# Rows of x in an interleaved order in an attention kernel, so that one DMA transpose turns a step's queries

## The reference, cut to what matters

```python
x: (4, 1024, 512)
xn = layernorm(x)
c_Q  = rms_norm(xn @ Wq_down);  c_KV = rms_norm(xn @ Wkv_down)
q_nop, q_pe = c_Q @ Wq_up, c_Q @ Wq_pe        # 16 heads of 128 and of 64 (rotary)
k_nop, v = split(c_KV @ Wkv_up)               # 8 key/value heads, each for 2 query heads
k_pe = rms_norm(xn @ Wk_pe)                   # rotary, one for all heads
scores = (q . k) * 192**-0.5, causal mask, softmax
y = attn @ v;  attn_out = y @ Wo
x_q = ternary(xn), w = ternary(weight) + rram;  ffn = x_q @ w.T
return x + attn_out + ffn
```

## Time and profile before

| | |
|---|---|
| median of 3 runs | 1703.25 us (1702.78 to 1703.85) |
| the profiled execution | 1702.12 us, span 1700.3 us |
| PE busy | 1633.8 us, 96% of the span |
| DVE, ACT, POOL busy | 1301.6, 1104.3, 580.3 us |
| DMA | 254.58 MB, mean 150 GB/s; queue of SP and ACT transposes and copies 80.3% of 16 engines' span |
| granted TensorE clock | 0.997 of full speed |

### The profile page before, as it was taken

How to read it: one execution, slowest core, us unless ns; L and a number is a source line. 1 busy time by engine, 2 the same in 40 slices (tenths; PEclk the granted TensorE clock), 3 DMA queues, 4 the chain that set the end, 5 groups by cost and what they waited for, 6 DMA issues and landing times.

```text
span 1700.3 us, 30407 instructions
## 1 busy us (share of the span) xinstructions
PE 1633.8 (96%) x9612; PEld 837.1 (49%) x9612; DVE 1301.6 (77%) x3369; ACT 1104.3 (65%) x2464; POOL 580.3 (34%) x1048
## 2 busy tenths in 40 slices
PE   4789999999999999999999999999999999999999
PEld 3445455544544445545454445554455444555444
DVE  5888878768688687777868787876868868777765
ACT  5877667567576666656666566756756666666663
POOL 3323334333343233433333333433333323333320
PEclk9999999999999999999999999999999999999999
DMA  9467988879979889987969988887987988998886
GB/s 259 97 103 141 150 147 154 147 134 158 152 138 161 145 152 159 166 149 122 161 126 167 170 148 147 154 149 129 161 153 141 159 144 151 162 159 147 147 153 126
DMA packets 914889, 254.58 MB, mean 150 GB/s; under 512 B 901608, under 2 KB 904042, under 8 KB 914410
## 3 DMA queue, kind: packets, MB, share of 16 engines
q1 hardware_dynamic: 904032, 228.98, 80.3%
q10 hardware_dynamic: 9162, 17.37, 3.3%
q0 software_dynamic: 1536, 6.29, 1.1%
HBM read 19.76 MB, written 8.39 MB: 17 GB/s over the span
## 4 chain that ended last, share of the span: by engine, by line
PE 71%; DMA 9%; issue 6%; ACT 5%; DVE 5%; SPq 2%; POOL 2%; ACTq 0%; DVEq 0%; POOLq 0%
DMA FT<-F 6%; PE bank L695 5%; PE bank L693 5%; PE bank L692 5%; PE bank L694 5%; PE bank L795 5%; PE bank L794 5%; PE bank L793 5%; PE bank L737 4%; PE bank L738 4%; PE bank L739 4%; PE bank L705 4%; ACT P L1082 2%; SPq L1848 2%; DVE F L1499 2%
## 5 line engine op out<-in xcount | busy, mean ns | idle before, releaser
L1082 ACT ACTIVATE P<-P,nm 128x256 f32<-128x256 f32 (+15 forms) x512 | 381.7, 746 | 439.6 <-DVE nm L1485 439.6
L1485 DVE CUSTOM_DVE_ANT_0 P<-bank,mask,neg 128x256 f32<-128x256 f32 (+15 forms) x512 | 383.0, 783 | 270.0 <-PE bank L705 261.8
L1719 POOL TENSOR_SCALAR sn<-sm 128x1 f32<-128x1 f32 x512 | 209.0, 409 | 926.1 <-ACT P L1082 918.6
L1077 ACT ACTIVATE F<-P,rc 128x256 f16<-128x256 f32 (+15 forms) x512 | 366.7, 743 | 101.0 <-DVE rc L1493 62.4
L1499 DVE SCALAR_TENSOR_TENSOR F<-P,rc,F 128x256 f16<-128x256 f32 (+15 forms) x512 | 401.6, 796 | 2.7 <-ACT F L1077 2.3
L692 PE MATMUL bank<-K,Q 128*128 128x512 f16 (+7 forms) x760 | 241.7, 319 | 0.8 <-DMA Q<-QS 0.8
L695 PE MATMUL bank<-K,Q 128*128 128x512 f16 (+7 forms) x760 | 241.7, 319 | 0.0
L693 PE MATMUL bank<-K,Q 128*128 128x512 f16 (+7 forms) x760 | 241.7, 319 | 0.0
L694 PE MATMUL bank<-K,Q 128*128 128x512 f16 (+7 forms) x760 | 241.7, 319 | 0.0
L793 PE MATMUL bank<-WO,YH 128*128 128x512 f16 x512 | 194.3, 379 | 4.0 <-DVE YL L1505 3.7
L794 PE MATMUL bank<-WO,YH 128*128 128x512 f16 x512 | 194.0, 379 | 0.0
(11 more groups left out here) (229 smaller groups left out, 2874.8 us busy)
## 6 DMA issues: line engine op xcount, KB each, us to landing
out<-X ACTq DMA_DIRECT2D x31, 256.0 KB, 3.6
X<-in_x ACTq DMA_DIRECT2D x28, 256.0 KB, 3.5
FT<-F SPq DMA_TRANSPOSE x348, 4.4
wo<-in_Wo POOLq DMA_DIRECT2D x4, 1024.0 KB, 7.0
Q<-QS SPq DMA_TRANSPOSE x256, 3.6
V<-CC SPq DMA_DIRECT2D x32, 64.0 KB, 3.0
X<-in_x SPq DMA_DIRECT2D x4, 256.0 KB, 8.4
kv<-in_Wkv_up POOLq DMA_DIRECT2D x1, 1024.0 KB, 12.5
```

The costliest lines, as they stand in the source:

```text
L1077: return e.eng.activation(dst, src, ACT.Copy, scale=scale)
L1082: e.eng.activation(m.P[:, u % 4, 0:w], m.P[:, u % 4, 0:w], ACT.Exp, bias=m.nm[:, u % 8:u % 8 + 1], scale=-1.0, accum_out=m.sm[:, u % 8:u % ...
L1485: e.eng.tensor_tensor_reduce(out=m.P[:, u % 4, 0:w], in0=m.pS[u % 2][:, off:off + w], in1=m.mask[:, end - w:end], scale=m.neg[:, :], scala ...
```

## The change

A tile's 128 rows are put on the partitions in another order: partition 2k + a holds row 64a + k of the tile (k from 0 to 63, a = 0 or 1). This is made where x is loaded, and undone where the output is stored, by the access pattern on the DRAM side; the rotary table is loaded in the same order, by two transfers in place of one.

- One DMA transpose turns all 128 partitions of `QS` (1,536 columns) into `Q`. A side's 128 weights are then every second column of two heads' 256.
- The causal mask and the products with `V` need keys in their natural order. The turned keys land in a new buffer `KT`, and POOL copies them to `K` in natural order (`keep_keys`, at g = 3 of tile t for tile t+2, behind the two units of p = 1; twice in the prologue). Scores wait for `k_at` of that copy in place of the transfer's `k_in`. The wait for the scores that still read the old keys moves from SP to POOL; SP waits for the copy of the tile before.
- `V` gets its natural order from two transfers of 64 partitions, each reading every second partition of `CC`.
- TensorE still writes `pY` in runs of 64, in natural order. The copies `values_hi` and `values_lo` write `YH` and `YL` with a step of two columns. They no longer multiply by 2^-4; the factor is put into the sum's scale (2^-12 for 2^-15) and the output's (2^-12 for 2^-11). In `values_lo` this makes a TENSOR_TENSOR of the SCALAR_TENSOR_TENSOR.

```diff
 def rows(dram, t):
-    return dram[b, i * 128:i * 128 + 128, :]
+    return by_places(dram[b, i * 128:i * 128 + 128, :])
+def by_places(dram):
+    return dram.rearrange("(a k) n -> k a n", a=2)
+def natural(values):
+    return values.rearrange("p (h a k) -> p h a k", a=2, k=64)
+def placed(values):
+    return values.rearrange("p (h k a) -> p h a k", a=2, k=64)
...
+        self.KT = own("KT", [128, 4, 128], F16)
-        self.Q = own("Q", [128, 2, 2, 768], F16)
+        self.Q = own("Q", [128, 2, 12, 128], F16)
...
     a, g = divmod(h, 2)
-    Q = m.Q[:, n % 2, a, :]
-    return [Q[:, 256 * x + 128 * g:256 * x + 128 * g + 128] for x in range(3)]
+    Q = m.Q[:, n % 2, :, :]
+    return [Q[:, 4 * x + 2 * g:4 * x + 2 * g + 2, :].rearrange("p h q -> p (h q)")[:, a::2] for x in range(3)]
...
-        e.wait_ge(s.q_in[p][n % 2], 16 * (n // 2 + 1))
-        e.wait_ge(s.k_in, 16 * (n // NG + 1))
+        e.wait_ge(s.q_in[n % 2], 16 * (n // 2 + 1))
+        e.wait_ge(s.k_at, n // NG + 1)
...
     def values_hi(n):
-        copy(m.YH[:, n % 2, :], m.pY[n % 2], 2.0 ** -4).then_inc(s.yh, 1)
+        copy(placed(m.YH[:, n % 2, :]), natural(m.pY[n % 2])).then_inc(s.yh, 1)
...
     def values_lo(n):
-        e.eng.scalar_tensor_tensor(out=m.YL[:, n % 2, :], in0=m.pY[n % 2], scalar=2.0 ** -4, in1=m.YH[:, n % 2, :],
-                                   op0=ALU.mult, op1=ALU.subtract).then_inc(s.yl, 1)
+        e.eng.tensor_tensor(placed(m.YL[:, n % 2, :]), natural(m.pY[n % 2]), placed(m.YH[:, n % 2, :]),
+                            ALU.subtract).then_inc(s.yl, 1)
...
+    def keep_keys(self, t):
+        at = key_slot(b, i) * 128
+        e.wait_ge(s.k_in, 16 * (t + 1))
+        if b:
+            e.wait_ge(s.wom, 16)
+        if b >= 2:
+            e.wait_ge(s.s, 4 * NG * (LAST_OF[b - 2] + 1))
+        e.eng.tensor_copy(m.K[:, :, at:at + 128].rearrange("p c (a k) -> p c a k", a=2),
+                          m.KT.rearrange("p c (k a) -> p c a k", a=2)).then_inc(s.k_at, 1)
...
 def gpsimd_attention(e, m, s, tiles, queries):
+            if (g, p) == (3, 1) and t + LEAD - 1 < T:
+                tiles.keep_keys(t + LEAD - 1)
...
     def keep(self, t):
         if t >= 2:
             e.wait_ge(s.up, NG * (t - 1))
+            e.wait_ge(s.k_at, t)
         if b >= 2:
-            e.wait_ge(s.s, 4 * NG * (LAST_OF[b - 2] + 1))
             e.wait_ge(s.pv, JBASE[NG * (LAST_OF[b - 2] + 1)])
-        e.eng.dma_start_transpose(out=m.K[:, :, at * 128:at * 128 + 128],
+        e.eng.dma_start_transpose(out=m.KT[:, :, :],
                                   in_=m.CC[:, 1, :, :].rearrange("p a n -> p (a n)")).then_inc(s.k_in, 16)
-        e.eng.dma_start(m.V[:, at, :, :], m.CC[:, 1, :, 0:128]).then_inc(s.v_in, 16)
+        for a in range(2):
+            e.eng.dma_start(m.V[64 * a:64 * a + 64, at, :, :], m.CC[a::2, 1, :, 0:128]).then_inc(s.v_in, 16)
...
     def turn_queries(n):
-        for a in range(2):
-            e.eng.dma_start_transpose(out=m.Q[:, n % 2, a, :].rearrange("p (c q) -> p c q", q=64),
-                                      in_=m.QS[64 * a:64 * a + 64, n % 2, :]).then_inc(s.q_in[a][n % 2], 16)
+        e.eng.dma_start_transpose(out=m.Q[:, n % 2, :, :], in_=m.QS[:, n % 2, :]).then_inc(s.q_in[n % 2], 16)
```

More of the change, by code:

```diff
@@ L339, in __init__ @@
         self.ld_x, self.st_o, self.xt_in = sems("ld_x", XSLOTS), sem("st_o"), sem("xt_in")
-        self.c_in, self.k_in, self.v_in = sem("c_in"), sem("k_in"), sem("v_in")
+        self.c_in, self.k_in, self.v_in, self.k_at = sem("c_in"), sem("k_in"), sem("v_in"), sem("k_at")
         self.const, self.wqs, self.nwq = sem("const"), sem("wqs"), sem("nwq")
@@ L360, in __init__ @@
         self.qh, self.ql, self.ph, self.pl = sem("qh"), sem("ql"), sem("ph"), sem("pl")
-        self.q_in = [sems("q_first", 2), sems("q_second", 2)]
+        self.q_in = sems("q_in", 2)
         self.s, self.mk, self.ex, self.sm, self.rc, self.fh, self.fl = (
@@ L714, in weigh_ready @@
             e.wait_ge(s.ft_in[z % FSLOTS], 16 * (z // FSLOTS + 1))
-        e.wait_ge(s.v_in, 16 * (n // NG + 1))
+        e.wait_ge(s.v_in, 32 * (n // NG + 1))
         if n >= 2:
@@ L927, in parts_hi @@
             e.wait_ge(s.k_in, 16 * t)
-            e.wait_ge(s.v_in, 16 * t)
+            e.wait_ge(s.v_in, 32 * t)
         self.copy(m.CC[:, 0, 0, 0:192], m.CR[:, 0:192], m.RM[:, 4, 0:1])
@@ L942, in queries_hi @@
         if n >= 2:
-            e.wait_ge(s.q_in[0][n % 2], 16 * (n // 2))
-            e.wait_ge(s.q_in[1][n % 2], 16 * (n // 2))
+            e.wait_ge(s.q_in[n % 2], 16 * (n // 2))
         e.eng.activation(m.QS[:, n % 2, 0:512], m.pU, ACT.Copy).then_inc(s.qh, 1)
@@ L1102, in last_values_hi @@
         e.wait_ge(s.c, N - 2)
-        copy(m.YH[:, (N - 1) % 2, 256 * p:256 * p + 256], m.pY[(N - 1 + p) % 2][:, 0:256], 2.0 ** -4).then_inc(s.yh, 1)
+        copy(placed(m.YH[:, (N - 1) % 2, 256 * p:256 * p + 256]), natural(m.pY[(N - 1 + p) % 2][:, 0:256])).then_inc(s.yh, 1)
     def load_x(t):
@@ L1122, in store_half @@
         at = slice(256 * k, 256 * k + 256)
-        e.eng.dma_start(rows(out, T - 1)[:, at], m.X[:, (T - 1) % XSLOTS, at]).then_inc(s.st_o, 16)
+        e.eng.dma_start(rows(out, T - 1)[:, :, at], m.X[:, (T - 1) % XSLOTS, at]).then_inc(s.st_o, 16)
     def outputs_out(o):
@@ L1469, in vector_prologue @@
     powers(slice(4, 5), m.G[:, 14:15])
-    e.eng.tensor_scalar(m.invo[:, :], m.IV[:, 4:5], 2.0 ** -11, None, ALU.mult).then_inc(s.sco, 1)
+    e.eng.tensor_scalar(m.invo[:, :], m.IV[:, 4:5], 2.0 ** -12, None, ALU.mult).then_inc(s.sco, 1)
     tiles.ffn_out(1, m.pY[0])
@@ L1511, in last_values_lo @@
         half = slice(256 * p, 256 * p + 256)
-        e.eng.scalar_tensor_tensor(out=m.YL[:, (N - 1) % 2, half], in0=m.pY[(N - 1 + p) % 2][:, 0:256], scalar=2.0 ** -4,
-                                   in1=m.YH[:, (N - 1) % 2, half], op0=ALU.mult, op1=ALU.subtract).then_inc(s.yl, 1)
+        e.eng.tensor_tensor(placed(m.YL[:, (N - 1) % 2, half]), natural(m.pY[(N - 1 + p) % 2][:, 0:256]),
+                            placed(m.YH[:, (N - 1) % 2, half]), ALU.subtract).then_inc(s.yl, 1)
     def accumulate(t):
@@ L1537, in vector_attention @@
     e.wait_ge(s.sco, 1)
-    e.wait_ge(s.ld_rope, 48)
+    e.wait_ge(s.ld_rope, 64)
     e.wait_ge(s.const, 10)
@@ L1653, in keys @@
         e.eng.tensor_tensor(lo, twice, hi, ALU.subtract).then_inc(s.kl, 1)
+    def keep_keys(self, t):
+        e, m, s = self.e, self.m, self.s
+        b, i = ORDER[t]
+        at = key_slot(b, i) * 128
[6 more added lines that the diff above has]
+                          m.KT.rearrange("p c (k a) -> p c a k", a=2)).then_inc(s.k_at, 1)
 class PoolQueries:
@@ L1697, in gpsimd_prologue @@
     e.eng.tensor_scalar(m.tern[:, :, :], m.fw[:, :, :], -0.2, None, ALU.is_lt).then_inc(s.tern, 1)
-    e.wait_ge(s.v_in, 16)
+    tiles.keep_keys(0)
+    e.wait_ge(s.v_in, 32)
     outputs.load(2)
@@ L1711, in gpsimd_prologue @@
     e.eng.memset(m.mask[:, 0:256], 0.0).then_inc(s.zero, 1)
+    tiles.keep_keys(1)
 def gpsimd_attention(e, m, s, tiles, queries):
@@ L1718, in scale_sum @@
             e.wait_ge(s.rc, u - 7)
-        e.eng.tensor_scalar(m.sn[:, u % 8:u % 8 + 1], m.sm[:, u % 8:u % 8 + 1], 2.0 ** -15, None,
+        e.eng.tensor_scalar(m.sn[:, u % 8:u % 8 + 1], m.sm[:, u % 8:u % 8 + 1], 2.0 ** -12, None,
                             ALU.mult).then_inc(s.sm, 1)
@@ L1809, in sync_prologue @@
     load_x(1)
-    e.eng.dma_start(m.rope[:, :, :, :], A["rope"].rearrange("(n p) a d -> p n a d", p=128)).then_inc(s.ld_rope, 16)
+    for a in range(2):
+        e.eng.dma_start(m.rope[a::2, :, :, :], A["rope"].rearrange("(n a k) x d -> a k n x d", a=2, k=64)[a]).then_inc(s.ld_rope, 16)
     e.eng.dma_start(m.mask[0:64, 960:1024], A["mask"][0:64, 0:64]).then_inc(s.ld_rope, 16)
```

1 line of the change is left out of this document (removed).

## The result

The changed kernel takes 1693.2 us (median of 4 runs, 1692.46 to 1695.74) against 1703.01 us for the kernel before (4 runs): ratio 0.9947, interval 0.993 to 0.9964, that is 9.0 us less (6.1 to 11.9; the two medians differ by 9.8). The forecast was 1688.5 in a range of 1678 to 1703. The profiled execution took 1692.72 us, its span is 1690.7 us. The same kernel run once more in the last batch of experiments gave 0.9943 (0.9922 to 0.9963).

The account below looks back on a forecast made before the run. TensorE's own products bound the kernel, its waits for DMA being the reachable part: 1702.1 - 16 + 0.7 + 0.5 = 1687.3 us for the profiled execution, so 1688.5 for the median of runs; range 1678 to 1703.

Parts of the forecast that it names:

- What bounds the kernel: TensorE, busy 96% of the span; without removing products, only its waits, 22.9 us of them for DMA, can be won.
- The size of the relief: TensorE's waits for transposes of probabilities and normalized rows: -16 us of 22.9 in 27 waits, bounds -5 and -23.
- the 70%: Share of the 22.9 us of DMA waits taken as recovered, with V's extra issue on SP's queue already allowed for.
- The DMA engines' time: Queries' transfer at full width: 0.64 to 1.10 us less in each of 128 steps, 82 to 141 us in all.
- SP's queue: One issue of 1.71 us for a step's queries in place of two taking 3.01 us: 1.3 us less per step.
- The 1.56 us near 908: Time SP's queue took after ACT's part was ready before issuing a transpose, read as a sign of a backed-up queue.
- Rival 4: Full-width transfer of queries no faster than its halves; gain about 2 us, 1701; chance 0.04.
- Rival 2: Strided weight loads in each unit's five products become the bound: 60 us more, 1749; chance 0.10.
- the 107 ns a load: Strided loads of Q without fast weight load: about 42 us higher, near 1730.
- Rival 3: Values' copies written in steps of two are slow: 37 us more, 1725; chance 0.04.
- Rival 1: Relief only moves TensorE's waits from FT to YL, leaving a quarter or less: 1699; chance 0.16.
- The small costs: First pair's queries +0.7 us, first key copy in the prologue +0.5 us; later key copies, 1.1 us on POOL, hidden.

Follow-up runs that it names:

- e1: Changed kernel, queries turned again by two transposes of 64 partitions each: 1714.89 us, ratio 1.0063 to the kernel before.
- e11: Kernel before, each tile's values copied by two transfers of 64 neighbouring partitions in place of one: 1707.3 us, ratio 1.0024.
- e12: Changed kernel, values' copies reading PSUM in steps, V issued by ACT from tile 2, normalized rows turned before probabilities at g = 2: 1737.94 us, ratio 1.0202.
- e13: As e12, with DVE's x_signs moved from g = 2, p = 0 to the end of g = 1, p = 1: 1695.86 us, ratio 0.9949.
- e2: Changed kernel, queries turned by two transposes of all 128 partitions and 768 columns each: 1706.33 us, ratio 1.0009 to the kernel before.
- e7: Changed kernel, keys turned straight into K in interleaved order, without POOL's copies (mask and values then don't fit): 1695.19 us, ratio 0.9944.
- e3: Changed kernel, values copied without the step of two, so output rows come in another order: 1692.57 us, ratio 0.9936.
- e5: Changed kernel, TensorE writing the values interleaved to PSUM in steps of two float32, copies plain: 2041.52 us, ratio 1.1972.
- e4: Changed kernel, values' copies written one column after the other and read from PSUM in steps of 64 float32: 1693.55 us, ratio 0.9937.

## Why the prediction was right, point by point

**What bounds the kernel.** Right. PE's waits for transposes were the reachable part; the waits for FT fell from 15.4 to 2.3 us, and the time by 9.0.

**The size of the relief.** I had -16 us, as 70% of 22.9 us in 27 waits. That sum was read wrongly: I took the loads' waits for further ones, and they are the same ones. In the kernel before, the product and its load wait together here:

```profile
1164.79 0.34 PE L450 MATMUL bank<-wdh,XT 128*128 128x384 f16 x1 [0.69 <-DMA XT<-XS]
```

```profile
1164.78 0.10 PEld L450 LDWEIGHTS bank<-wdh,XT 128*128 128x128 f16 x1 [1.18 <-DMA XT<-XS]
```

The product ahead starts at 1163.71, so the two starts lie 1.08 us apart where 0.21 is the pace: 0.87 us are lost, and the product's row has 0.69, because its predecessor is recorded at 0.38 us. So the products' rows alone are to be counted, with some 0.17 us for each wait (an estimate from this one): 18.3 + 21 x 0.17 = 21.9 us in 21 waits. That the wrong sum came so near is luck. In the same way 7.5 us are left after (8 waits), 11.8 in the second profile (13 waits): 14.4 and 10.1 us less, for the 16 forecast. The waits for DVE rose from 8.5 to 13.1 and 12.9 us. The nets, -9.8 and -5.7, fit the spans, which are 9.6 and 6.8 us shorter. The runs say the same: from e1 to the change it is 20 us; about 3 of them are e1's own waits for Q, so against the kernel before some 17, and less V's second issue, which I had put into the 70%, some 13. The term had the right place and nearly the right size.

What failed are the costs beside it, which I had put at nothing or inside it: V costs some 4 us (e11), the copies at most 2. With them e1's 10.7 us over the kernel before are 4 + 2 + 3 = 9; the rest of some 2 us lies within the intervals and stays open. XT's waits, of the same queue, I had counted as relieved; they rose from 2.9 to 3.8 us, and to 6.1 in the second profile, and e12 and e13 show that XT's input, DVE's signs of x, is late.

**The DMA engines' time.** I had 0.64 to 1.10 us less per step, 82 to 141 us. It was 1365 - 1317 = 48 us, 0.38 us per step. The error was in reading: 215 GB/s was seen at a DMA share of 1.14, 159 at 1.00, and I divided bytes by GB/s alone. With the share, 1.83 x 1.14 = 2.09 against 2.47 us, the difference is 0.38 us, what was measured; the row of 287 GB/s, at a share of 1.28, would still have given too much, 0.72. The share of queue 1 fell by 2.4 points, from 80.3% to 77.9%, and not by 5 to 8. The Trainium skill ("SBUF — State Buffer", Door 1: The DMA port swizzle) says that partitions 0 to 63 reach only half of the ports, and gives 196 against 328 GB/s for plain transfers of 1 MiB. The runs agree in kind, 159 against 214 GB/s.

**SP's queue.** I had 1.3 us less per step: 3.01 to 1.66 is 1.35. That one issue less is worth 11 us by itself, with the engines' time unchanged, I had not said; e2 shows it. The 1.56 us near 908 that I read as a queue backed up show no such thing: they are the issue itself, and these 348 issues take 1.76 us in the median.

**Rivals.** Rival 4 (no faster full-width) is out by the window and e2. Rival 2 (strided loads) is out by the 29 ns between products, and with it the 107 ns a load that I weighed. Rival 3 (slow strided copies) is real in kind, +151 and +48 ns, not +580 and +680, and worth at most 2 us. Rival 1 (the relief only moves the waits) explains little: of 12.2 us that the products no longer wait for FT and XT, 3.9 came back as waits for QS and YL, and most of these 3.9 are no answer to the relief. With plain copies (e3) the row of YL is again that of the kernel before:

```profile
PE bank L812 <- DVE YL L1522: 3.7, 9, 0.6
```

so its 1.0 us is the price of the copies. And QS, 2.4 us before and 5.3 after, is at 4.2 already in e1, where FT is not relieved at all; why, the runs don't show.

**The small costs.** For the first pair's queries I had +0.7 us; products wait 0.4 us for Q in the changed kernel, less than before, so nothing. `keep_keys` I had at 1.1 us on POOL, hidden; it takes 620 ns, and e7 shows it hidden. The +0.5 us of the prologue is too small for e7, which leaves out those two copies too.

## What to carry to other kernels

Where several engines' transposes share one issuing queue, count its issues as work of its own: here one transfer less in each step, with the same time of the DMA engines, was worth 11 us. Look for what the reorder needs at its seams: a second small transfer in front of a crowded queue cost some 4 us, a copy on an engine that is busy for a third of the time cost nothing. A product and its weight load wait for the same thing, so don't add their rows. When rates are read from windows, divide the engines' share out before comparing them. And when an experiment that should part two causes is read, look at what else it changed: e2 was built to keep two issues, and its issues were shorter.

## What the runs showed of the hardware

TensorE loads 128 float16 weights from every second column as fast as from neighbouring ones (29 ns between products of 64 columns). It writes PSUM in steps of two float32 at half the pace of runs of 64 columns (0.43 against 0.21 us for 512 columns, e5). ACT takes 151 ns more for 512 float16 written in steps of two (730 for 579). DVE takes 48 ns more when one float16 operand is read and the output written so (729 for 681). Neither takes more for reading PSUM in steps of 64 columns (578 and 681, e4). An issue of a DMA transpose holds SP's queue for 1.66 us in the median with 128 partitions and 1,536 columns, 1.47 with 64 partitions, 1.29 with 128 partitions and 768 columns; that of a plain copy of 64 partitions for 0.61.
